# Softmax sums of an attention kernel: GpSimd adds three of a group's four tiles of exponentials, TensorE sums the fourth itself

## What is computed

```python
cond = silu(c) @ wc.T + bc                 # shift, scale and gate, twice
h = ln(x) * (1 + sc1) + sh1
q, k, v = h @ wq.T, h @ wk.T, h @ wv.T     # 4 groups x 4 query heads x 32
a = softmax(q k^T / sqrt(32)); x = x + g1 * ((a v) @ wo.T)
h = ln(x) * (1 + sc2) + sh2
x = x + g2 * (gelu(h @ w1.T + b1) @ w2.T + b2)
```

## Time and profile before

| | |
|---|---|
| median of 3 runs | 1500.6 us (1500.55 to 1503.28) |
| the profiled execution, its own time | 1506.23 us |
| its span, first to last instruction | 1504.5 us |
| TensorE clock granted over the span | 0.984 of full speed |
| TensorE busy | 1447.9 us, 96% |
| VectorE, ScalarE, GpSimd busy | 800.1, 621.3, 577.0 us |

### The profile page before, as it was taken

One profiled execution on the slowest core, in us unless ns is written; L12 is line 12 of the kernel. 1 busy time (PEld: TensorE's weight loads), 2 busy tenths in 40 slices (PEclk: granted clock), 3 DMA queues, 4 the chain that ended last, 5 costly groups with the idle time before them and its releaser, 6 DMA issues. The chain is left out here.

```text
span 1504.5 us, 19118 instructions
## 1 busy us (share of the span) xinstructions
PE 1447.9 (96%) x6989; PEld 1048.7 (70%) x6989; DVE 800.1 (53%) x1360; ACT 621.3 (41%) x1118; POOL 577.0 (38%) x224
## 2 busy tenths in 40 slices
PE   6899999999999999999799999999999999999996
PEld 5655666656666566655378878787887878878785
DVE  6877777776777677776334432424224242332421
ACT  6376657585766667575333212121121122112110
POOL 1067587776778586877200020202002020120202
PEclk9999999999999999999899999999999999999998
DMA  8232422323232324221342220200102010010100
GB/s 296 61 82 53 111 55 82 98 80 115 82 108 78 103 54 124 66 83 39 105 149 83 77 64 1 91 0 28 63 0 91 0 64 27 28 63 0 63 1 28
DMA packets 68388, 105.15 MB, mean 70 GB/s; under 512 B 10504, under 2 KB 19736, under 8 KB 68320
## 3 DMA queue, kind: packets, MB, share of 16 engines
q1 hardware_dynamic: 68320, 104.27, 22.6%
HBM read 55.44 MB, written 16.81 MB: 48 GB/s over the span
## 5 line engine op out<-in xcount | busy, mean ns | idle before, releaser
L824 DVE TENSOR_REDUCE neg_max<-row_bank 128x1 f32<-128x512 f32 x512 | 337.6, 683 | 146.8 <-PE row_bank L1062 142.3
L1500 PE MATMUL acc<-w_t,hidden 128*128 128x512 f32 x1536 | 370.8, 391 | 7.7 <-DVE hidden L1417 7.7
L1490 PE MATMUL up<-h,w_t 128*128 128x512 f32 x1536 | 371.2, 392 | 0.0
L668 ACT ACTIVATE probs<-key_bank 128x512 f32<-128x512 f32 x512 | 299.6, 597 | 169.1 <-PE key_bank L1075 163.8
L1500 PEld LDWEIGHTS acc<-w_t,hidden 128*128 128x128 f32 x1536 | 287.3, 188 | 69.9 <-DVE hidden L1417 10.7
L1490 PEld LDWEIGHTS up<-h,w_t 128*128 128x128 f32 x1536 | 287.6, 188 | 58.7
L1415 DVE CAST hidden<-gelu_full 128x512 fp32r<-128x512 f32 x128 | 67.4, 527 | 443.8 <-ACT gelu_full L1361 442.2
L1361 ACT ACTIVATE gelu_full<-up,bias_cols 128x512 f32<-128x512 f32 x128 | 88.3, 690 | 515.3 <-PE up L1490 515.3
L547 POOL TENSOR_TENSOR probs_sum<-probs_sum,probs 128x2048 f32<-128x2048 f32 x62 | 285.4, 4603 | 15.6 <-ACT probs L668 9.3
L1075 PE MATMUL key_bank<-q_stack,k_stack 98*128 98x512 f32 x512 | 221.3, 435 | 4.2 <-ACT probs L668 3.9
L1318 POOL TENSOR_TENSOR y<-y,gate_now 128x512 f32<-128x512 f32 x32 | 47.4, 1482 | 454.9 <-DVE y L1425 454.9
(11 more groups left out here) (133 smaller groups left out, 1066.0 us busy)
## 6 DMA issues: line engine op xcount, KB each, us to landing
q_stack<-spare SPq DMA_DIRECT2D x384, 64.0 KB, 2.0
xa<-in_x_dram SPq DMA_DIRECT2D x8, 1024.0 KB, 9.4
resid<-in_x_dram SPq DMA_DIRECT2D x8, 1024.0 KB, 7.0
x_scratch<-resid SPq DMA_DIRECT2D x8, 1024.0 KB, 4.5
xa<-x_scratch SPq DMA_DIRECT2D x8, 1024.0 KB, 5.8
spare<-in_L_cond_w_dram SPq DMA_DIRECT2D x32, 256.0 KB, 3.0
resid<-x_scratch SPq DMA_DIRECT2D x8, 1024.0 KB, 6.8
out_dram<-y SPq DMA_DIRECT2D x8, 1024.0 KB, 4.2
```

Source lines behind the costliest of these rows:

```text
L668: nc.scalar.activation(probs[kt][:, r, :], key_bank[r % 2][:, :], ACT.Exp).then_inc(exp_done, 1)
L824: nc.vector.tensor_reduce(out=neg_max[:, g % 2, i:i + 1], in_=row_bank[(g + i) % 2][:, :], op=ALU.max, axis=AX.X, negate=True).then_inc(ro ...
L1490: last = nc.tensor.matmul(up[j % 2][:, :], w1_t[i][:, kt, j * P:j * P + P], h[k][:, kt, :], start=(kt == 0 and n == 0), stop=(kt == KD - 1 ...
L1500: last = nc.tensor.matmul(acc[tt][:, :], hidden[j % 2][i][:, tt * P:tt * P + P], w2_t[k][:, j, :], start=(j == 0 and n == 0), stop=(j == N ...
```

## The change

GpSimd makes two additions in a group (tiles 0, 1 and 2). The fourth tile, `probs3`, is not added; TensorE multiplies it by ones itself and accumulates it on top of `probs_sum` in the same bank. The same holds for the last group, whose additions are VectorE's. ScalarE, which waited for the third addition ahead of overwriting `probs3`, now waits for the sums of the group before.

```diff
+        ADDS = TT - 2
+        def adds_no(b, g):
+            return group_no(b, g) * ADDS
+        def adds_in(b):
+            return ADDS
...
-                            for kt in range(1, TT):
+                            for kt in range(1, adds_in(b) + 1):
                                 add_probs(b, g, kt)
...
                         act.wait_ge(pv_done, tile_no(b, g, kt) - (TT - 1))
-                        act.wait_ge(added, group_no(b, g) * (TT - 1) - (TT - 1) + max(kt, 1))
+                        last = (b, g - 1) if g > 0 else (b - 1, HKV - 1)
+                        if kt <= adds_in(last[0]):
+                            act.wait_ge(added, adds_no(*last) + max(kt, 1))
+                        else:
+                            act.wait_ge(sums_ready, group_no(b, g))
...
-                    if g == HKV - 1 and not has_next and kt > 0 and r == R - 1:
+                    if g == HKV - 1 and not has_next and 0 < kt <= adds_in(b) and r == R - 1:
                         add_probs(b, g, kt)
...
                 def sums(b, g, is_first=False):
-                    pe.wait_ge(added, group_no(b, g) * (TT - 1) + (TT - 1))
+                    pe.wait_ge(added, adds_no(b, g) + adds_in(b))
                     if not is_first:
                         pe.wait_ge(attn_split, group_no(b, g))
-                    for r in range(R):
-                        last = nc.tensor.matmul(sum_bank[HD * r:HD * r + HD, :], ones[:, :], probs_sum[:, r, :],
-                                                start=True, stop=True)
+                    summed = [probs_sum] + ([probs[TT - 1]] if adds_in(b) < TT - 1 else [])
+                    if len(summed) > 1:
+                        pe.wait_ge(exp_done, exps_no(b, g, TT - 1) + R)
+                    for i, tile in enumerate(summed):
+                        for r in range(R):
+                            last = nc.tensor.matmul(sum_bank[HD * r:HD * r + HD, :], ones[:, :], tile[:, r, :],
+                                                    start=(i == 0), stop=(i == len(summed) - 1))
```

More of the change, by code:

```diff
@@ L544, in add_probs @@
                     if kt > 1:
-                        pool.wait_ge(added, group_no(b, g) * (TT - 1) + (kt - 1))
+                        pool.wait_ge(added, adds_no(b, g) + (kt - 1))
                     first_in = probs[0] if kt == 1 else probs_sum
@@ L855, in add_probs @@
                     else:
-                        dve.wait_ge(added, group_no(b, g) * (TT - 1) + (kt - 1))
+                        dve.wait_ge(added, adds_no(b, g) + (kt - 1))
                     dve.wait_ge(exp_done, exps_no(b, g, kt) + R)
```

## The result

The changed kernel takes 1527.5 us (median of 4 runs, 1525.9 to 1528.6), the kernel before 1501.9 us in the same comparison (4 runs). The ratio is 1.0168, 95% interval 1.0150 to 1.0186: 25.5 us slower by the medians, 25.2 us by the ratio (22.5 to 27.9). The forecast was 1526.9 us and 26.3 us.

What follows compares the result with a forecast made beforehand. TensorE was taken as the bound: 27.8 us for the tiles, less 0.2 for GpSimd's relief and 1.3 for the gate's waits, gave 26.3 us on 1500.6, so 1526.9 us; own range 1523 to 1532, overall 1519 to 1533.

Steps and rivals of the forecast that it cites:

- TensorE is the bound, and the tile is paid in full: Attention: TensorE is busy nearly throughout, nothing covers the added tile in 32 groups, 27.8 us.
- The price, 0.87 us from the value products: Sums of each group: the added tile costs 0.87 us, like a value-product tile of the same shape.
- The higher end, 0.97: Sums of each group: upper price if the second tile too pays a step to another shape, 31.0 us in all.
- No new wait costs: Attention: the sums' wait for the fourth tile's exponentials and ScalarE's wait for the previous group's sums cost nothing.
- GpSimd's relief, 0.2 us: Attention: dropping 31 additions of 4.60 us gains only the 0.2 us TensorE waited, once, for one.
- The waits for the gate, 1.3 us: A few beats behind a sum, twice: TensorE's waits behind VectorE's for the gate's transfer go, 1.3 us.
- The median and the profiled execution: Whole kernel: fixed added work, so the 26.3 us goes on the median 1500.6 us, 5.6 us below the profiled execution.
- TensorE's waits: Rival, attention: all 6.7 us of TensorE's waits go and take part of the tile, 1521.7 us; chance 0.08.
- The clock: Rival, three low-clock stretches of attention: more work keeps the clock up, 1518.9 us, or one more stretch, 1530.3 us; chance 0.08.
- GpSimd's queue sets the sums: Rival, sums after the input-row transfer: one addition fewer saves up to 32.2 us of TensorE's wait, 1496.2 us; chance 0.02.
- VectorE did not get faster from the relief: VectorE's row maxima in attention: fewer GpSimd additions free nothing there, 0.
- the column places don't overlap: Rival, sums: accumulating matmuls run one behind the other, eight instructions 4.75 us, 152 us in all, 1653 us; chance 0.02.

Runs made afterwards that it cites:

- two tiles: Against the changed kernel, GpSimd makes one addition in a group and TensorE sums tiles 2 and 3 itself: 1556.0 us, ratio 1.0339 to before.
- cheaper sums: Against the kernel before, GpSimd's third addition writes a bf16 tile and TensorE sums that with bf16 ones: 1484.6 us, ratio 0.9872.
- the relief alone: Against the changed kernel, fourth tile left out of the sums, bias of 1 in the logarithm: 1501.6 and 1500.3 us, ratios 0.9983 and 0.9972 to before.

## Why the prediction came out right, point by point

**TensorE is the bound, and the tile is paid in full.** Right, and shown for the seven sequences before the last: one tile and two tiles lengthen a middle sequence by 3.5 and 6.9 us, cheaper sums shorten it, and the waits of ScalarE and VectorE take up the time.

**The price, 0.87 us from the value products.** Right: 0.86 us in the timeline, 0.86 from the sequences (3.45 / 4). The higher end, 0.97, was the tile with the step to another shape, which is paid once.

**No new wait costs.** Right. Neither TensorE's wait for the fourth tile's exponentials nor ScalarE's for the sums appears in the waits.

**GpSimd's relief, 0.2 us.** The place was right, the second group of the last sequence, and in the middle sequences the relief is worth nothing. The size was read from the list of waits, which is short of it: the landmarks of before hold 0.4 us at that place, because a matmul's busy time runs on past the moment at which the next could start (two value tiles are 1.92 us busy and 1.74 us apart from the sums). The timed runs of the relief alone are 2.6 and 4.2 us faster. That this is the relief isn't shown: keeping the third addition beside the tile made no difference that the runs could tell (1530.6 and 1531.1 us), and the kernels that keep it are as far below their sum as the others. Where these 2 to 3 us come from is open.

**The waits for the gate, 1.3 us.** The number went, and the reason has more for it than against it. I took them for a lag that a longer beat hides. VectorE waits for this transfer in attention in none of the five traces with the tile in all sequences; in those with the beat as before twice, twice and three times not at all; and with the shorter bf16 sums three, five and four times. So the lag grows as the beat gets shorter, as the prediction has it. But at the beat of before it is there only in some executions, so 1.3 us is the size of one execution and not of the median. Without the term the forecast would have been 1528.2 us, also near.

**The median and the profiled execution.** I put the difference on the median of three runs, 1500.6 us, and left the 5.6 us between them open. Against the later medians (1504.4 to 1505.3 us) the profiled execution was nearly ordinary, and the first three runs were low; that the time was met to 0.6 us is therefore partly luck: the median of before rose by 1.3 us with a fourth run, and the difference was 0.8 us smaller than forecast. The difference itself is what the prediction stands on. The spans of the two profiled executions (19.6 us apart) would have made the change look cheaper than it is.

**The rivals.** TensorE's waits did not take part of the tile beyond the gate's: they are 1.0 us less, and both waits behind the gate's transfer are gone. The clock did not rise with more matmuls over the whole: the granted clock of the changed kernel's four runs is 0.984 to 0.988, and in one of its two traces looked at closely the low stretch at the start of the last sequence was there, in the other not. The rule of the Trainium skill that activity lifts the low clock (TensorE: Matmul & The Clock Gate, Part 1) does not bring the 8.0 us of that rival here. In the middle sequences the granted clock is 1.00 before and after, so there is nothing to lift. Only the third step of the last sequence looks like it, 0.91 in both changed traces where it was 0.82, which is worth 1.7 us. That GpSimd's queue sets the sums was wrong for this kernel, and right as a mechanism: with bf16 sums it appears, at the second group of a sequence, where the earlier trace rows had shown the small margin. VectorE did not get faster from the relief: its row maxima take 683 ns on average in the changed kernel, as before. The fourth, that the column places don't overlap, is refuted by the 0.86 us of the second tile.

## What to carry to other kernels

Relief of an engine is worth what the bound engine waits for it, and work moved onto the bound engine is paid one for one; the wait list in both directions and the timeline of one place gave the difference within a microsecond or two of 25. Effects of 3 us and less the timed runs of this kernel show only in part, and here they do not add up. If the sums are to become cheaper, make them cheaper on the engine that is the bound: one pass in bf16 gained some 20 us where the move lost 25, at the price of less exact sums, and then the margins of what lies in shadow (GpSimd's third addition, 0.06 us at one group, and the transfer of the gate) decide what is left. One profiled execution carries several microseconds of chance: don't count a wait that appears twice in 32 groups at its full size until a second trace has it, and look for it again when the work around it gets shorter.

## What I had not expected of the hardware

Four column-placed matmuls of 512 columns take 0.86 us in fp32 with two instructions each and 0.33 us in bf16 with one each, the step to the next shape included (0.97 in fp32). The same code runs with one low-clock stretch more or less from execution to execution: 20.7 or 21.8 us (the change in the last sequence only) and 21.6 or 24.2 us (the changed kernel) for the first step of the last sequence.
